# Matrix transposes written as products with the identity, in a graph network kernel

## The chip, the cores and the metric

One core of one Trainium2 chip runs the whole program. The metric is the time of one execution on the device in microseconds (us). The engines are called PE (TensorE), DVE (VectorE), ACT (ScalarE), POOL (GpSimd) and SP (SyncE, which only issues transfers here). PEld is PE's weight load, which the profile lists beside the products.

## The reference

Two message passing layers over a graph of 6250 nodes and 206250 edges, sorted by the node that they end in. A node has 64 scalars and 32 vectors of 3 components (160 numbers). All is float32.

```python
# layer 0, per edge (attention)
msg_s = (s_n @ Ws_src)[src] + (s_n @ Ws_dst)[dst]          # and the same for the vectors
w1 = rbf @ W_rbf                                           # 16 -> 224, the radial product
m1_s, m1_v = _cg_tp(msg_s, msg_v, y0, y1, w1[...])         # products with y0, y1: outer, dot, cross
a = (m1_s @ W_alpha).reshape(e, H, AS_)                    # the logits, softmax over the edges of a node
val_s, val_v = m1_s @ Ws_val, einsum(m1_v, Wv_val) * sigmoid(val_s @ Wg)
m2_s, m2_v = _cg_tp(sigmoid(val_s), val_v, y0, y1, w2...)
h = concat(m2_s @ Ws_vlin, einsum(m2_v, Wv_vlin))
agg = segment_sum(alpha * h, dst)                          # then node + agg @ Wps, Wpv, and a norm
# layer 1, per edge (convolution)
w = edge_query @ tp_weight                                 # 64 -> 224
edge_x = products of w, h[edge_src] and edge_sh            # 352 numbers (outer, dot, cross)
agg = segment_sum(edge_x, edge_dst)                        # then two linear maps, and a norm
```

## The kernel before

The program runs seven stages one after the other, each a block with its own instruction streams. Their order by time is: `attention_input` (norm of the nodes and the two tables that edges gather from, 49 blocks of 128 nodes), `attention_edges` (404 groups of 512 edges), `segment_softmax`, `attention_aggregate` (452 steps), `attention_output` (49 blocks), `conv_edges` (452 steps of 512 edges), `conv_output` (49 blocks).

Features of edges or nodes lie with the edge or node on the partition. To multiply them by a weight matrix, PE needs them turned, with the feature on the partition. So each such product is preceded by PE transposes of 128 rows into PSUM, and by a copy of the turned block to SBUF on ACT.

In `attention_edges` the work on one group of 512 edges (four sub-blocks k of 128 edges) is spread over several passes of a loop body. PE's body, in the order of the code, is: `turn(t,0)`, `values_of(t,0)`, `turn(t,1)`, `turn(t,2)`, `values_of(t,1)`, `maps(t,0)`, `turn2(t,0)`, the radial product (L681), `turn2(t,1)`, `maps(t,1)`, `turn2(t,2)`, where the t of each belongs to another group of edges. Each `turn` (L614) and `turn2` (L623) is four transposes, one for each k. `maps` (L631 to L633) is six products with 200, 96 and 96 columns twice over; `values_of` (L641 to L643) is six products with 96 columns. ACT copies each turned block of 128 by 512 (L709, L713). DVE adds the gathered rows (L570), forms outer products with y (L498, L550), cross and dot products (L512 to L527), and multiplies with the radial weights in PSUM (L531 to L540, after which `first_done` goes up). PE's radial product waits for `first_done` of the group before, since `b_w` is not double buffered. DVE forms `rbfy` (L521) from two halves of a loaded tile `rin`.

In `conv_edges` PE sums the edges of a node by products with a 0/1 matrix (L1331, L1333) and multiplies the queries (L1343). DVE does the outer products with y in three instructions on line L1269 (diag, plus, minus), the cross and dot products (L1283 to L1285), a copy of y to PSUM (L1290), and more. Nothing there is transposed.

All waits are written out by hand with semaphores. Each engine takes its instructions in the order of the code.

Of the kernel before, what the change touches and what calls it, by code (L numbers as in the profile page):

```python
# [21 lines left out]
ALU = mybir.AluOpType  # L22
# [5 lines left out]
P = 128  # L28
# [20 lines left out]
    ("ones", 128, 128), ("count", 128, STEPS), ("sidx", 128, 4),  # L49
    ("iota", 128, 128), ("wy", 64, WY), ("m1_0", 128, 200), ("m1_1", 128, 96), ("m1_2", 96, 96), ("val_t", 64, 128),  # L50
# [97 lines left out]
def attention_input(nc, g):  # L148
# [6 lines left out]
    with ExitStack() as ctx:  # L155
# [27 lines left out]
        with nc.Block() as block:  # L183
# [155 lines left out]
            @block.tensor  # L339
            def _(pe):  # L340
                pe.wait_ge(chain, 4)
                for c in range(4):
                    ins = pe.matmul(banks[6][:, 0:STEPS], w("ones"), begun[:, c, :], start=(c == 0), stop=(c == 3))
                ins.then_inc(summed, 1)
                for m in range(BLOCKS + 1):
                    if m < BLOCKS:
                        pe.wait_ge(phase, 8 * chunk_of[m] + 8)
                        wait(pe, kept, m - 1)
                        pe.transpose(b_t[m % 2][0:CS, 0:P], normed[:, m, 0:CS], w("ident"))
                        pe.transpose(b_t[m % 2][0:V3, P:2 * P], normed[:, m, CS:C], w("ident")).then_inc(turned, 1)  # L350
# [12 lines left out]


def attention_edges(nc, g):

    w, psum, banks, io = g["w"], g["psum"], g["banks"], g["io"]
    with ExitStack() as ctx:
# [10 lines left out]
        gdst = [sb(f"gdst{u}", [P, 4, C]) for u in range(4)]  # L379
        rin = [sb(f"rin{u}", [64, 512]) for u in range(4)]  # L380
        rbfy = [sb(f"rbfy{u}", [64, 256]) for u in range(2)]
        msg = sb("msg", [P, 4, C])
# [46 lines left out]
        with nc.Block() as block:  # L429
# [47 lines left out]
            def _(dve):  # L477
# [10 lines left out]
                def body(m):  # L488
# [26 lines left out]
                    if t.inside(SUPER):  # L515
                        dve.wait_ge(early_in[t.slot4], 16 * (t.quarter + 1))
                        wait(dve, outer_done, t.n)
                        dve.tensor_copy(ya, y_early[t.slot4][:, :, 1:6]).then_inc(ya_done, 1)
                        dve.wait_ge(rin_in[t.slot4], 16 * (t.quarter + 1))
                        wait(dve, pe_weights, t.n - 1)  # L520
                        dve.tensor_tensor(rbfy[t.slot][:, :], rin[t.slot4][:, 0:256], rin[t.slot4][:, 256:512], ALU.mult)\  # L521
                            .then_inc(spread, 1)
# [87 lines left out]
            def _(pe):  # L610
                def turn(t, b):
                    lo, rows = P * b, V3 if b == 2 else P
                    for k in range(4):
                        ins = pe.transpose(b_t[b % 2][0:rows, P * k:P * k + P], first[t.slot][:, k, lo:lo + rows], w("ident"))  # L614
                    ins.then_inc(pe_turned, 1)

                def turn2(t, b):
                    for k in range(4):
                        if b < 2:
                            what = second[t.slot][:, k, P * b:P * b + P]  # L620
                        else:
                            what = gated[t.slot4][:, k, 8:12, :].rearrange("p b c -> p (b c)")
                        ins = pe.transpose(b_t[(b + 1) % 2][:, P * k:P * k + P], what, w("ident"))  # L623
                    ins.then_inc(pe_turned2, 1)
# [21 lines left out]
                def body(m):  # L646
# [29 lines left out]
                    if t.inside(SUPER):  # L676
                        pe.wait_ge(spread, t.n + 1)
                        wait(pe, first_done, t.n)
                        for k in (0, 2, 1, 3):
                            q, e = 32 * (k // 2), P * (k % 2)  # L680
                            ins = pe.matmul(b_w[:, k, :], rbfy[t.slot][q:q + 32, e:e + P], w("wy")[q:q + 32, :], start=True, stop=True)  # L681
                        ins.then_inc(pe_weights, 1)
# [331 lines left out]
def attention_output(nc, g):  # L1014
# [3 lines left out]
    with ExitStack() as ctx:  # L1018
# [18 lines left out]
        with nc.Block() as block:  # L1037
# [88 lines left out]
            def _(pe):  # L1126
                for m in range(BLOCKS + LAG + 1):
                    b = m
                    if b < BLOCKS:
                        pe.wait_ge(shared, 3 * (b // 7) + 3)  # L1130
                        wait(pe, u_kept, b - 1)
                        pe.transpose(bt_u[b % 2][0:V3, 0:P], agg[:, b, 0:V3], w("ident"))
                        pe.transpose(bt_u[b % 2][0:V3, P:2 * P], agg[:, b, CS:C], w("ident")).then_inc(u_turned, 1)
                    b = m - LAG
                    if 0 <= b < BLOCKS:
                        pe.wait_ge(phase, 8 * (b // 7) + 8)
                        wait(pe, t_kept, b - 1)
                        pe.transpose(bt_t[b % 2][0:V3, 0:P], nodes[:, b, 0:V3], w("ident"))
                        pe.transpose(bt_t[b % 2][0:V3, P:2 * P], nodes[:, b, CS:C], w("ident")).then_inc(t_turned, 1)
                    b = m - 1  # L1140
# [44 lines left out]
def conv_edges(nc, g):  # L1185
# [3 lines left out]
    with ExitStack() as ctx:  # L1189
# [6 lines left out]
        idx = [idx_ring[:, u] for u in range(8)]  # L1196
        y_ring = sb("y", [P, 8, 4, 6])
        y = [y_ring[:, u] for u in range(8)]
# [7 lines left out]
        plain = [sb(f"plain{u}", [P, 4, P]) for u in range(4)]  # L1206
        diag, plus = sb("diag", [P, 4, 3, CV]), sb("plus", [P, 4, 3, CV])
        cross, dot = sb("cross", [P, 4, 3, CV]), sb("dot", [P, 4, CV])
# [8 lines left out]
        minus = banks[6][:, 0:384].rearrange("p (k x c) -> p k x c", k=4, x=3)  # L1217
        yp = [banks[6][:, 384 + 24 * u:408 + 24 * u].rearrange("p (k j) -> p k j", k=4) for u in range(2)]
        iota = banks[7][:, 0:P]
# [4 lines left out]
        with nc.Block() as block:  # L1224
            @block.sync
            def _(sp):
                def body(t):

                    step_loads(sp, t, g["step_s"], ((scaled, t.n - 7), (weights, t.n - 7), (plain_done, t.n - 7)),
                               ((idx[t.slot8][:, :], io["eidx"], loaded[t.slot8]),  # L1230
                                (y[t.slot8][:, :, :].rearrange("p k j -> p (k j)"), io["ey6"], loaded[t.slot8]),
                                (query[t.slot8][:, :], io["query"], loaded[t.slot8])))
# [15 lines left out]
            def _(dve):  # L1248
# [4 lines left out]
                def body(m):  # L1253
                    t = m
                    if t.inside(STEPS):
# [31 lines left out]
                    if t.inside(STEPS):  # L1287
                        dve.wait_ge(loaded[t.slot8], 48 * (t.eighth + 1))
                        wait(dve, outer_done, t.n - 1)
                        dve.tensor_copy(yp[t.slot], y[t.slot8][:, :, :]).then_inc(turned_y, 1)  # L1290
                        wait(dve, summed, t.n - 3)
# [57 lines left out]
def conv_output(nc, g):  # L1349

    w, banks, agg, nodes, io = g["w"], g["banks"], g["agg1"], g["nodes"], g["io"]
    with ExitStack() as ctx:
# [12 lines left out]
        with nc.Block() as block:  # L1365
# [94 lines left out]
def lay_pack(i):  # L1460
# [12 lines left out]
    ss, sv, vs, vv0, vv1 = rbf[:, :64], rbf[:, 64:128], rbf[:, 128:160], rbf[:, 160:192], rbf[:, 192:224]  # L1473
    for lo in (0, 32):
        W["wy"][lo:lo + 16, 0:64], W["wy"][lo:lo + 16, 192:224] = ss, vs
        W["wy"][lo + 16:lo + 32, 64:128], W["wy"][lo + 16:lo + 32, 128:160], W["wy"][lo + 16:lo + 32, 160:192] = sv, vv0, vv1
    for name in ("gamma_s", "beta_s"):
# [42 lines left out]
def lay_inputs(i):  # L1520
# [15 lines left out]

    rbf = np.pad(np.asarray(i["edge_attr_16"]), ((0, E - EDGES), (0, 0))).reshape(SUPER, 2, 256, 16).transpose(0, 1, 3, 2)
    y0 = np.broadcast_to(y[:, :, 0].reshape(SUPER, 2, 1, 256), rbf.shape)
    left = np.concatenate([rbf, rbf], 2).reshape(SUPER, 64, 256)
    right = np.concatenate([y0, np.ones_like(rbf)], 2).reshape(SUPER, 64, 256)  # L1540
    query = np.pad(np.asarray(i["edge_attr_64"]), ((0, E - EDGES), (0, 0))).reshape(SUPER, 2, 256, 64)
    query = query.transpose(0, 1, 3, 2).reshape(SUPER, P, 256)
    return dict(
        pack=lay_pack(i), x=x, eidx=eidx, ey6=ey6, sdst=sdst, dst3=dst3,
        rin=np.concatenate([left, right], 2), yall=y.reshape(4 * SUPER, P, 4).transpose(1, 0, 2),
# [21 lines left out]
```

## Time and profile before

| what | value |
|---|---|
| median of 3 runs | 7991.2 us (7987.54 to 7993.15) |
| profiled execution | 7987.12 us, of which its span 7985.3 us |
| DVE busy | 7640.4 us, 96% of the span |
| PE busy | 7044.2 us, 88% |
| PE weight loads | 5904.8 us, 74% |
| ACT busy | 5259.3 us, 66% |
| POOL busy | 5304.9 us, 66% |
| mean granted clock of PE | 0.967 of 2.4 GHz |

The span runs from the first to the last instruction; the execution is 1.8 us longer. PE busy counts the modelled ends of pipelined matmuls, so it is more than the time in which the array takes columns: the starts of successive matmuls tell the rate. Shares over the whole span are means over seven stages, so the stages are looked at one by one.

### The profile page before, as it was taken

How to read it: one execution, taken by the hardware profiler on the slowest of the kernel's cores; microseconds unless marked ns; L12 is line 12 of the kernel's file. 1: busy time of each engine (PE TensorE's matmuls, PEld its weight loads, DVE VectorE, ACT ScalarE, POOL GpSimd, SP SyncE). 2: the span in 40 equal slices, each digit the busy share in tenths (PEclk: the TensorE clock that was granted, in tenths of full speed). 3: DMA queues.
4: the chain of work that ended last, by engine and by line, in shares of the span. 5: the costliest groups of instructions: out<-in, count | busy, mean ns of one | idle time of the engine just before them, and what ended most of it. 6: DMA issues, size and time to landing. Idle time of an engine off the chain costs nothing. (4 is left out here: it accounts for less than half of the span.)

```text
span 7985.3 us, 199893 instructions
## 1 busy us (share of the span) xinstructions
PE 7044.2 (88%) x48227; PEld 5904.8 (74%) x48227; DVE 7640.4 (96%) x19067; ACT 5259.3 (66%) x18286; POOL 5304.9 (66%) x5500
## 2 busy tenths in 40 slices
PE   6899999999999999999999859998888888888888
PEld 4888888888888888888888848875555555555556
DVE  5999999999999999999999889976999999999999
ACT  2666666666666666666666634435777777777775
POOL 2777777777777777777777426634777777777772
PEclk5999999999999999999999979977999999999999
DMA  3444344433443333443333337732333333333332
GB/s 104 107 109 105 105 106 105 106 105 104 106 105 106 105 105 106 105 106 105 105 106 106 84 130 261 258 115 69 93 89 90 89 89 88 89 89 89 90 89 58
DMA packets 789804, 854.44 MB, mean 107 GB/s; under 512 B 413920, under 2 KB 571488, under 8 KB 789216
## 3 DMA queue, kind: packets, MB, share of 16 engines
q0 software_dynamic: 241920, 413.20, 21.2%
q1 hardware_dynamic: 547232, 436.34, 18.3%
q10 hardware_dynamic: 576, 4.01, 0.1%
q8 instruction: 33, 0.54, 0.0%
q14 instruction: 43, 0.35, 0.0%
HBM read 704.54 MB, written 148.44 MB: 107 GB/s over the span
## 5 line engine op out<-in xcount | busy, mean ns | idle before, releaser
L1242 POOL DMA_INDIRECT agg<-tab_conv,ce_idx x1808 | 1708.7, 945 | 866.5 <-issue 616.0
L468 POOL DMA_INDIRECT ae_gsrc<-tab_src,ae_idx x1616 | 1533.5, 949 | 751.3 <-issue 446.9
L471 POOL DMA_INDIRECT ae_gdst<-tab_dst,ae_idx x1616 | 1645.9, 1019 | 539.6 <-issue 539.6
L1331 PE MATMUL psum<-ce_prod,ce_plain 128*128 128x384 f32 x3616 | 1539.7, 508 | 328.5 <-DVE ce_prod L1304 275.7
L1316 ACT ACTIVATE ce_prod<-ce_raw,ce_y 128x64 f32<-128x64 f32 x5424 | 1463.8, 332 | 0.0
L1314 ACT ACTIVATE ce_prod<-ce_raw,ce_y 128x160 f32<-128x160 f32 x1808 | 752.2, 416 | 514.5 <-DVE ce_raw L1263 514.5
L713 ACT ACTIVATE ae_second_t<-psum 128x512 f32<-128x512 f32 x1212 | 732.1, 604 | 507.3 <-PE psum L623 500.1
L1333 PEld LDWEIGHTS psum<-ce_prod,ce_plain 128*128 128x128 f32 x3616 | 687.7, 190 | 479.5 <-issue 1.5
L1331 PEld LDWEIGHTS psum<-ce_prod,ce_plain 128*128 128x128 f32 x3616 | 546.9, 191 | 475.4 <-DVE ce_plain L1292 345.5
L631 PE MATMUL psum<-pack_sb,ae_first_t 128*128 128x200 f32 x3232 | 850.1, 345 | 2.2 <-ACT ae_first_t L709 2.0
L641 PE MATMUL psum<-pack_sb,ae_second_t 128*128 128x96 f32 x3232 | 664.4, 287 | 129.1 <-ACT ae_second_t L713 126.6
L709 ACT ACTIVATE ae_first_t<-psum 128x512 f32<-128x512 f32 (+1 forms) x1212 | 692.1, 610 | 41.1 <-PE psum L614 40.9
L681 PE MATMUL psum<-pack_sb,ae_rbfy 32*128 32x224 f32 x3232 | 417.4, 372 | 303.0 <-DVE ae_first L540 281.2
L641 PEld LDWEIGHTS psum<-pack_sb,ae_second_t 128*128 128x128 f32 x3232 | 486.0, 190 | 241.4 <-issue 164.0
L614 PE MATMUL psum<-pack_sb,ae_first 128*128 128x128 f32 (+1 forms) x4848 | 662.9, 273 | 0.8 <-ACT ae_first_t L709 0.8
L719 ACT ACTIVATE ae_values<-psum 128x256 f32<-128x256 f32 x808 | 310.2, 384 | 522.2 <-PE psum L643 522.2
L1333 PE MATMUL psum<-ce_prod,ce_plain 128*128 128x96 f32 x3616 | 646.8, 261 | 0.0
L948 POOL TENSOR_TENSOR ag_exval<-ag_val,ag_wide 128x384 f32<-128x384 f32 x452 | 385.2, 852 | 381.3 <-DMA ag_val<-h_dram 190.7
L633 PE MATMUL psum<-pack_sb,ae_first_t 96*128 96x96 f32 x3232 | 625.9, 275 | 0.0
L643 PE MATMUL psum<-pack_sb,ae_second_t 128*128 128x96 f32 x3232 | 625.4, 275 | 0.0
L642 PE MATMUL psum<-pack_sb,ae_second_t 128*128 128x96 f32 x3232 | 625.3, 275 | 0.0
L765 ACT ACTIVATE ae_second<-agg,ae_y_late 128x192 f32<-128x192 f32 x1616 | 598.3, 444 | 0.0
(217 smaller groups left out, 18692.7 us busy)
## 6 DMA issues: line engine op xcount, KB each, us to landing
ag_val<-h_dram SPq DMA_DIRECT2D x452, 320.0 KB, 4.1
h_dram<-ae_hout SPq DMA_DIRECT2D x404, 320.0 KB
agg<-in_query SPq DMA_DIRECT2D x452, 128.0 KB
ae_rin<-in_rin SPq DMA_DIRECT2D x404, 128.0 KB
agg<-tab_conv,ce_idx POOLq DMA_INDIRECT x1808
ae_gsrc<-tab_src,ae_idx POOLq DMA_INDIRECT x1616
ae_gdst<-tab_dst,ae_idx POOLq DMA_INDIRECT x1616
ce_idx<-in_eidx SPq DMA_DIRECT2D x452, 4.0 KB
```

Source lines behind the costliest of these rows:

```text
L468: pool.indirect_dma_start(gsrc[t.slot4][:, k, :], None, g["tab_src"], bass.IndirectOffsetOnAxis(ap=idx[t.slot4][:, k:k + 1], axis=0))\
L471: pool.indirect_dma_start(gdst[t.slot4][:, k, :], None, g["tab_dst"], bass.IndirectOffsetOnAxis(ap=idx[t.slot4][:, 4 + k:5 + k], axis=0))\
L614: ins = pe.transpose(b_t[b % 2][0:rows, P * k:P * k + P], first[t.slot][:, k, lo:lo + rows], w("ident"))
L631: pe.matmul(b_m[:, i, 0:200], first_t[0][:, e], w("m1_0"), start=True, stop=False)
L641: pe.matmul(b_h[:, i, 0:96], second_t[0][:, e], w("m2_0"), start=True, stop=False, skip_group_check=True)
L709: act.activation(first_t[b][0:rows, :], b_t[b % 2][0:rows, :], ACT.Copy).then_inc(kept, 1)
L713: act.activation(second_t[b][:, :], b_t[(b + 1) % 2][:, :], ACT.Copy).then_inc(kept2, 1)
L1242: pool.indirect_dma_start(node[t.slot8][:, k, :], None, g["tab_conv"], bass.IndirectOffsetOnAxis(ap=idx[t.slot8][:, k:k + 1], axis=0))\
L1314: act.activation(prod[t.slot][:, k, 0:160], raw[t.slot][:, k, 0:160], ACT.Identity, scale=y[t.slot8][:, k, 0:1])
L1316: ins = act.activation(prod[t.slot][:, k, 192 + 96 * x:256 + 96 * x], raw[t.slot][:, k, 160:WW], ACT.Identity, scale=y[t.slot8][:, k, x + ...
L1331: pe.matmul(b_a[t.slot], plain[t.slot4][:, k, :], prod[t.slot][:, k, 96:480], start=(k == 0), stop=False, skip_group_check=True)
L1333: ins = pe.matmul(b_a[t.slot][:, 96:384].rearrange("p (x c) -> p x c", x=3)[:, :, CS:96], plain[t.slot4][:, k, :], prod[t.slot][:, k, 0:96 ...
```

## The change

Every `pe.transpose` outside of `segment_softmax` becomes `pe.matmul` with the same operands: the data as stationary matrix and the identity as moving one. The radial product takes `rbfy` from 128 partitions instead of 64: two sub-blocks of 128 edges share the columns, and each reads its weights from its own rows and its own half of a wider `wy`, in which the other rows are zero. In `conv_edges` the products for diag and plus are one DVE instruction, for which y is loaded with eight numbers per edge (a new input `ey8`) instead of six.

```diff
-                        pe.transpose(b_t[m % 2][0:CS, 0:P], normed[:, m, 0:CS], w("ident"))
+                        pe.matmul(b_t[m % 2][0:CS, 0:P], normed[:, m, 0:CS], w("ident"), start=True, stop=True)
...
-        rin = [sb(f"rin{u}", [64, 512]) for u in range(4)]
-        rbfy = [sb(f"rbfy{u}", [64, 256]) for u in range(2)]
+        rin = [sb(f"rin{u}", [P, 2 * P]) for u in range(4)]
+        rbfy = [sb(f"rbfy{u}", [P, P]) for u in range(2)]
...
-                        dve.tensor_tensor(rbfy[t.slot][:, :], rin[t.slot4][:, 0:256], rin[t.slot4][:, 256:512], ALU.mult)\
+                        dve.tensor_tensor(rbfy[t.slot][:, :], rin[t.slot4][:, 0:P], rin[t.slot4][:, P:2 * P], ALU.mult)\
...
-                        ins = pe.transpose(b_t[b % 2][0:rows, P * k:P * k + P], first[t.slot][:, k, lo:lo + rows], w("ident"))
+                        ins = pe.matmul(b_t[b % 2][0:rows, P * k:P * k + P], first[t.slot][:, k, lo:lo + rows], w("ident"), start=True, stop=True)
...
-                        ins = pe.transpose(b_t[(b + 1) % 2][:, P * k:P * k + P], what, w("ident"))
+                        ins = pe.matmul(b_t[(b + 1) % 2][:, P * k:P * k + P], what, w("ident"), start=True, stop=True)
...
-                            q, e = 32 * (k // 2), P * (k % 2)
-                            ins = pe.matmul(b_w[:, k, :], rbfy[t.slot][q:q + 32, e:e + P], w("wy")[q:q + 32, :], start=True, stop=True)
+                            q, half = slice(64 * (k // 2), 64 * (k // 2) + 64), WY * (k % 2)
+                            ins = pe.matmul(b_w[:, k, :], rbfy[t.slot][q, :], w("wy")[q, half:half + WY], start=True, stop=True)
...
-                        pe.transpose(bt_u[b % 2][0:V3, 0:P], agg[:, b, 0:V3], w("ident"))
+                        pe.matmul(bt_u[b % 2][0:V3, 0:P], agg[:, b, 0:V3], w("ident"), start=True, stop=True)
...
-                        pe.transpose(bt_t[b % 2][0:V3, 0:P], nodes[:, b, 0:V3], w("ident"))
+                        pe.matmul(bt_t[b % 2][0:V3, 0:P], nodes[:, b, 0:V3], w("ident"), start=True, stop=True)
...
-        diag, plus = sb("diag", [P, 4, 3, CV]), sb("plus", [P, 4, 3, CV])
+        both = sb("both", [P, 4, 2, 3, CV])
+        diag, plus = both[:, :, 0, :, :], both[:, :, 1, :, :]
...
-                        for d, out in enumerate((diag[:, :, :, :], plus[:, :, :, :], minus)):
-                            ins = dve.tensor_tensor(out, comps(here[:, :, CS:C]),
-                                                    yp[t.slot][:, :, 1 + d:4 + d].unsqueeze(3).to_broadcast(three), ALU.mult)
-                        ins.then_inc(outer_done, 1)
+                        dve.tensor_tensor(both[:, :, :, :, :].rearrange("p k d x c -> p k d (x c)"),
+                                          here[:, :, CS:C].unsqueeze(2).to_broadcast([P, 4, 2, V3]),
+                                          yp[t.slot][:, :, 0:6].unsqueeze(3).to_broadcast([P, 4, 6, CV]), ALU.mult)
+                        dve.tensor_tensor(minus, comps(here[:, :, CS:C]), yp[t.slot][:, :, 4:7].unsqueeze(3).to_broadcast(three),
+                                          ALU.mult).then_inc(outer_done, 1)
...
-                            ins = pe.transpose(b_t[b % 4][:, P * i:P * i + P], agg[:, b, P * i:P * i + P], w("ident"))
+                            ins = pe.matmul(b_t[b % 4][:, P * i:P * i + P], agg[:, b, P * i:P * i + P], w("ident"), start=True, stop=True)
```

## Rows read from the trace of the kernel before

**Rows 1.** Windows by stage: length, busy time (and instructions) of each engine, granted PE clock, DMA.

```profile
0.00:163.00 163.00, 108.64 (x304) 67.33 (x304) 84.53 (x180) 36.84 (x108) 23.01 (x15) 0.56 0.32 110
163.00:4590.00 4427.00, 4002.96 (x32333) 3687.77 (x32334) 4335.58 (x11313) 2943.88 (x8891) 3172.25 (x3225) 0.99 0.40 104
...
5278.00:5475.00 197.00, 186.52 (x596) 134.21 (x594) 88.65 (x199) 53.73 (x155) 15.78 (x1) 0.51 0.07 22
5475.00:7908.00 2433.00, 2104.06 (x10848) 1434.39 (x10848) 2420.16 (x5876) 1920.96 (x7232) 1708.70 (x1808) 1.00 0.37 88
7908.00:7985.30 77.30, 55.66 (x441) 53.83 (x441) 61.66 (x114) 24.27 (x57) 0.00 (x0) 0.84 0.13 53
```

**Rows 2.** Waits, 1000 to 4000: who waited, for whom, us in total, times, longest.

```profile
PE psum L681 <- DVE ae_first L540: 185.2, 277, 0.8
...
PE psum L641 <- ACT ae_second_t L713: 85.6, 276, 0.3
```

**Rows 3.** Timeline of `attention_edges`, PE's products alone: start, us, what, count.

```profile
2999.91 1.03 PE L681 MATMUL psum<-pack_sb,ae_rbfy 32*128 32x224 f32 x8 [0.61 <-DVE ae_first L540]
...
3002.92 0.60 PE L623 MATMUL psum<-pack_sb,agg 128*128 128x128 f32 x4
...
3003.36 0.60 PE L614 MATMUL psum<-pack_sb,ae_first 128*128 128x128 f32 x4
...
3004.29 0.46 PE L641 MATMUL psum<-pack_sb,ae_second_t 128*128 128x96 f32 x2 [0.33 <-ACT ae_second_t L713]
...
3005.70 1.04 PE L614 MATMUL psum<-pack_sb,ae_first 128*128 128x128 f32 x8
...
3006.57 0.39 PE L641 MATMUL psum<-pack_sb,ae_second_t 128*128 128x96 f32 x2
...
3007.92 0.53 PE L631 MATMUL psum<-pack_sb,ae_first_t 128*128 128x200 f32 x2
...
3009.49 0.60 PE L623 MATMUL psum<-pack_sb,ae_second 128*128 128x128 f32 x4
...
3010.91 1.03 PE L681 MATMUL psum<-pack_sb,ae_rbfy 32*128 32x224 f32 x8 [0.81 <-DVE ae_first L540]
```

**Rows 4.** Groups by line and shape, whole span: count, busy, mean ns, idle before.

```profile
L614 PE MATMUL psum<-pack_sb,ae_first 128*96 128x128 f32 x1616 | 243.0, 273 | 0.8 <-ACT ae_first_t L709 0.8
...
L643 PE MATMUL psum<-pack_sb,ae_second_t 128*128 128x96 f32 x3232 | 625.4, 275 | 0.0
...
L1008 PE MATMUL psum<-ag_exval,ag_hot 128*128 128x164 f32 x3616 | 568.4, 313 | 18.2 <-DVE ag_exval L987 13.0 <-issue 0.2
```

**Rows 5.** Timelines of `attention_aggregate` and `conv_edges`, PE's products.

```profile
5274.77 4.26 PE L1008 MATMUL psum<-ag_exval,ag_hot 128*128 128x164 f32 x27
...
6502.48 0.84 PE L1331 MATMUL psum<-ce_prod,ce_plain 128*128 128x384 f32 x2
...
6503.16 0.36 PE L1333 MATMUL psum<-ce_prod,ce_plain 128*128 128x96 f32 x2
...
6505.18 1.03 PE L1343 MATMUL psum<-pack_sb,agg 64*128 64x224 f32 x8
```

**Rows 6.** Timeline of `conv_edges`, DVE: start, us, what.

```profile
6501.01 0.27 DVE L1304 TENSOR_TENSOR ce_prod<-psum,ce_dot 128x128 f32<-128x128 f32 x1
6501.20 0.67 DVE L1260 TENSOR_TENSOR ce_raw<-psum,agg 128x512 f32<-128x512 f32 x1
6501.80 0.54 DVE L1263 TENSOR_TENSOR ce_raw<-psum,agg 128x384 f32<-128x384 f32 x1
```

**Rows 7.** Timeline of PE where `attention_edges` begins, at the lower clock.

```profile
183.36 2.89 PE L614 MATMUL psum<-pack_sb,ae_first 128*128 128x128 f32 x12
...
192.21 1.86 PE L681 MATMUL psum<-pack_sb,ae_rbfy 32*128 32x224 f32 x8 [1.92 <-DVE ae_first L540]
```

**Rows 8.** Windows there (columns as in the first group): the granted clock rises.

```profile
196.00:197.00 1.00, 1.00 (x6) 1.00 (x6) 0.00 (x0) 0.00 (x0) 0.69 (x2) 0.50 0.19 50
...
198.00:199.00 1.00, 0.69 (x6) 0.45 (x5) 0.79 (x2) 0.96 (x3) 0.80 (x1) 1.00 0.51 98
```

More of the change, by code:

```diff
@@ L49 @@
     ("ones", 128, 128), ("count", 128, STEPS), ("sidx", 128, 4),
-    ("iota", 128, 128), ("wy", 64, WY), ("m1_0", 128, 200), ("m1_1", 128, 96), ("m1_2", 96, 96), ("val_t", 64, 128),
+    ("iota", 128, 128), ("wy", 128, 2 * WY), ("m1_0", 128, 200), ("m1_1", 128, 96), ("m1_2", 96, 96), ("val_t", 64, 128),
     ("wg", 64, 32), ("adot", 128, 72), ("m2_0", 128, 96), ("m2_1", 128, 96), ("m2_2", 128, 96),
@@ L348, in _ @@
                         wait(pe, kept, m - 1)
-                        pe.transpose(b_t[m % 2][0:CS, 0:P], normed[:, m, 0:CS], w("ident"))
-                        pe.transpose(b_t[m % 2][0:V3, P:2 * P], normed[:, m, CS:C], w("ident")).then_inc(turned, 1)
+                        pe.matmul(b_t[m % 2][0:CS, 0:P], normed[:, m, 0:CS], w("ident"), start=True, stop=True)
+                        pe.matmul(b_t[m % 2][0:V3, P:2 * P], normed[:, m, CS:C], w("ident"), start=True, stop=True).then_inc(turned, 1)
                     b = m - 1
@@ L1131, in _ @@
                         wait(pe, u_kept, b - 1)
-                        pe.transpose(bt_u[b % 2][0:V3, 0:P], agg[:, b, 0:V3], w("ident"))
-                        pe.transpose(bt_u[b % 2][0:V3, P:2 * P], agg[:, b, CS:C], w("ident")).then_inc(u_turned, 1)
+                        pe.matmul(bt_u[b % 2][0:V3, 0:P], agg[:, b, 0:V3], w("ident"), start=True, stop=True)
+                        pe.matmul(bt_u[b % 2][0:V3, P:2 * P], agg[:, b, CS:C], w("ident"), start=True, stop=True).then_inc(u_turned, 1)
                     b = m - LAG
@@ L1137, in _ @@
                         wait(pe, t_kept, b - 1)
-                        pe.transpose(bt_t[b % 2][0:V3, 0:P], nodes[:, b, 0:V3], w("ident"))
-                        pe.transpose(bt_t[b % 2][0:V3, P:2 * P], nodes[:, b, CS:C], w("ident")).then_inc(t_turned, 1)
+                        pe.matmul(bt_t[b % 2][0:V3, 0:P], nodes[:, b, 0:V3], w("ident"), start=True, stop=True)
+                        pe.matmul(bt_t[b % 2][0:V3, P:2 * P], nodes[:, b, CS:C], w("ident"), start=True, stop=True).then_inc(t_turned, 1)
                     b = m - 1
@@ L1196, in conv_edges @@
         idx = [idx_ring[:, u] for u in range(8)]
-        y_ring = sb("y", [P, 8, 4, 6])
+        y_ring = sb("y", [P, 8, 4, 8])
         y = [y_ring[:, u] for u in range(8)]
@@ L1217, in conv_edges @@
         minus = banks[6][:, 0:384].rearrange("p (k x c) -> p k x c", k=4, x=3)
-        yp = [banks[6][:, 384 + 24 * u:408 + 24 * u].rearrange("p (k j) -> p k j", k=4) for u in range(2)]
+        yp = [banks[6][:, 384 + 28 * u:412 + 28 * u].rearrange("p (k j) -> p k j", k=4) for u in range(2)]
         iota = banks[7][:, 0:P]
@@ L1230, in body @@
                                ((idx[t.slot8][:, :], io["eidx"], loaded[t.slot8]),
-                                (y[t.slot8][:, :, :].rearrange("p k j -> p (k j)"), io["ey6"], loaded[t.slot8]),
+                                (y[t.slot8][:, :, :].rearrange("p k j -> p (k j)"), io["ey8"], loaded[t.slot8]),
                                 (query[t.slot8][:, :], io["query"], loaded[t.slot8])))
@@ L1289, in body @@
                         wait(dve, outer_done, t.n - 1)
-                        dve.tensor_copy(yp[t.slot], y[t.slot8][:, :, :]).then_inc(turned_y, 1)
+                        dve.tensor_copy(yp[t.slot], y[t.slot8][:, :, 1:8]).then_inc(turned_y, 1)
                         wait(dve, summed, t.n - 3)
@@ L1473, in lay_pack @@
     ss, sv, vs, vv0, vv1 = rbf[:, :64], rbf[:, 64:128], rbf[:, 128:160], rbf[:, 160:192], rbf[:, 192:224]
-    for lo in (0, 32):
-        W["wy"][lo:lo + 16, 0:64], W["wy"][lo:lo + 16, 192:224] = ss, vs
-        W["wy"][lo + 16:lo + 32, 64:128], W["wy"][lo + 16:lo + 32, 128:160], W["wy"][lo + 16:lo + 32, 160:192] = sv, vv0, vv1
+    for lo in (0, 32, 64, 96):
+        own = W["wy"][lo:lo + 32, WY * (lo // 32 % 2):]
+        own[0:16, 0:64], own[0:16, 192:224] = ss, vs
+        own[16:32, 64:128], own[16:32, 128:160], own[16:32, 160:192] = sv, vv0, vv1
     for name in ("gamma_s", "beta_s"):
@@ L1535, in lay_inputs @@
     ey6 = y.reshape(SUPER, 4, P, 4)[..., [0, 1, 2, 3, 1, 2]].transpose(0, 2, 1, 3).reshape(SUPER, P, 24)
[L1537 to L1540, printed above, removed]
+    ey8 = y.reshape(SUPER, 4, P, 4)[..., [0, 1, 2, 3, 2, 3, 1, 2]].transpose(0, 2, 1, 3).reshape(SUPER, P, 32)
+    rbf = np.pad(np.asarray(i["edge_attr_16"]), ((0, E - EDGES), (0, 0))).reshape(SUPER, 4, P, 16).transpose(0, 1, 3, 2)
+    y0 = np.broadcast_to(y[:, :, 0].reshape(SUPER, 4, 1, P), rbf.shape)
+    left = np.concatenate([rbf, rbf], 2).reshape(SUPER, P, P)
+    right = np.concatenate([y0, np.ones_like(rbf)], 2).reshape(SUPER, P, P)
     query = np.pad(np.asarray(i["edge_attr_64"]), ((0, E - EDGES), (0, 0))).reshape(SUPER, 2, 256, 64)
@@ L1543, in lay_inputs @@
     return dict(
-        pack=lay_pack(i), x=x, eidx=eidx, ey6=ey6, sdst=sdst, dst3=dst3,
+        pack=lay_pack(i), x=x, eidx=eidx, ey6=ey6, ey8=ey8, sdst=sdst, dst3=dst3,
         rin=np.concatenate([left, right], 2), yall=y.reshape(4 * SUPER, P, 4).transpose(1, 0, 2),
```

## The prediction

> **What bounds the kernel now.** I cut the span into its stages first [rows 1], since a share over the whole span hides who waits. `attention_edges` is more than half of it: 4427 us, in which DVE is busy for 4336 us (98%) and PE for 4003 us (90%). DVE sets the pace and PE is close behind. `conv_edges` is 2433 us with DVE busy for 2420 us. `attention_input` (163 us) and `attention_output` (197 us) run with a mean granted clock of 0.56 and 0.51, so PE is mostly at its lower level of 1.2 GHz, and in `attention_output` PE is busy for 187 of 197 us. `conv_output` has both levels (mean 0.84). The aggregation and the softmax aren't touched.
>
> The list of waits names two on PE in `attention_edges`: for DVE's `first_done` before the radial product, 185 us, and for ACT's copy before `values_of`, 86 us [rows 2]. The first comes once in each group of 512 edges, 277 times in 3000 us, so a group takes 10.83 us. To see how much room PE has I took one group from the timeline and went by starts, since the durations contain pipelined ends [rows 3]. From one radial product to the next it is 11.00 us there. Four transposes take 0.44 us (3002.92 to 3003.36) and eight take 0.87 us, so PE stood idle from 3003.80 to 3004.29 and from 3009.93 to 3010.91, 1.47 us. PE's own work is 11.00 - 1.47 = 9.53 us a group. Of it the 24 transposes are 24 x 0.11 = 2.64 us, and the rest 6.89 us.
>
> **The change, part by part.**
>
> *Transposes in `attention_edges`.* A transpose leaves one matmul record: the third block of `first`, 4 x 404 = 1616 transposes, shows x1616. A plain float32 product leaves two: L643, also 1616 in the code, shows x3232 [rows 4]. So each turned block becomes two passes, each with its weight load. What a pass with 128 moving columns costs no row at full clock shows. From below: passes with 96 columns follow each other in (3007.92 - 3006.57)/12 = 0.1125 us [rows 3], closer to the 0.11 us of a transpose than to their columns, so the weight load of 128 columns, the same here, is what they wait for. From above: 164 columns take (4.26 - 0.31)/26 = 0.152 us, with 0.31 us for the end of the last; 384 columns take (6503.16 - 6502.48)/2 = 0.34 us [rows 4, 5]. The line through these two falls by 0.00085 us a column and gives 0.152 - 36 x 0.00085 = 0.121 us at 128. That is above the bound of the load, so I take it. The 48 passes are 5.81 us, and PE's work is 6.89 + 5.81 = 12.70 us a group.
>
> DVE needs 10.83 us less what is saved below, so PE becomes the bound. Its old stalls go. The four transposes of `turn(t,0)` now last 0.97 us and cover ACT's copy (0.77 us from the end of `turn2` at 3003.52 to the start of `values_of` at 3004.29). `first_done` comes before PE needs it, since DVE has 1.9 us to spare in each group. So a group takes 12.70 us: 404 x (12.70 - 10.83) = **+755 us**. At 0.1125 us a pass it is 6.89 + 5.40 = 12.29 us and +590 us; at 0.152 us it is 14.19 us and +1357 us.
>
> The Trainium skill (TensorE: Matmul & The Clock Gate, section Terms) says of the transpose mode that it is four times faster for FP32. That speaks against this change more strongly than the rows do, which give 0.242 against 0.11 us, a factor of 2.2. By the page's factor a turned block would take 0.44 us and the stage 2675 us more.
>
> *Radial product.* `rbfy` goes from 256 to 128 elements a partition. In DVE's timeline 128 elements take 0.19 us to the next start and 512 take 0.60 us [rows 6], so 128 elements less are 0.137 us, 55 us over 404 groups. With PE as the bound they are hidden in DVE's new idle time: 0. They count if DVE stays the bound. On PE nothing: eight passes with 64 rows and 224 columns in `conv_edges` take 1.03 us [rows 5], as the eight with 32 rows do [rows 3]. The transfers have the same bytes over twice the partitions, at a DMA share of 0.40 [rows 1].
>
> *y products merged in `conv_edges`.* Two instructions of 384 elements become one of 768. By rows 6 the fixed part of one is 0.19 - 0.137 = 0.05 to 0.06 us, and 452 x 0.06 = **-27 us**, all of it on the path, since DVE is busy for 99% of the stage [rows 1]. The copy of y grows by 4 elements, 2 us in all; the loads of y are 4 KB larger, against a DMA share of 0.37. Bounds: 0 and -40 us.
>
> *`conv_output`.* 147 transposes become 294 passes. PE's part grows by 147 x (0.242 - 0.11) = 19 us, but DVE is busy for 62 of 77 us [rows 1] and PE waits part of the time: **+10 us**, between 0 and 25 us.
>
> *`attention_input` and `attention_output`.* Here the clock decides. At 1.2 GHz a transpose takes twice its 0.11 us (twelve are in 2.89 us with the end of the last [rows 7]), and a second pass another 0.22 us, so 98 blocks add 22 us and 196 add 43 us, nearly all on PE's path. But where `attention_edges` begins, PE did 12 transposes from 183.36 us and the granted clock was still 0.50 at 196 us; after the run of plain products that begins at 192.21 us it had gone to 1.00 by 198 us [rows 7, 8]. With the transposes gone both stages are nothing but plain products, so I expect the upper level for most of them. In `attention_output` PE's work of 187 + 43 us would halve to 115 us, beside 89 us of DVE and hand-overs to ACT that don't shrink; I take 150 us, **-45 us**. In `attention_input` PE's 109 + 22 us would become 65 us, less than DVE's 85 us [rows 1]; of the 163 us I take off **-30 us**.
>
> The Trainium skill (same page, Part 4: PE-mode transpose) says that transposes don't engage the upper clock level, because they aren't counted as PE being busy. The start of `attention_edges` agrees. With the rule these two stages give -75 us, without it +65 us.
>
> *Sum.* 755 - 27 + 10 - 30 - 45 = +663 us against the profiled execution's 7987.1 us (2 us over its span, 4 under the median): 8650, with the median 8654. I say **8650 us**.
>
> **Rivals.**
> 1. *The same, but the clock stays low in the two node stages.* For it: both run at the lower level although most of their passes are plain already. The sum is 755 - 27 + 10 + 22 + 43 = +803, 8790 us.
> 2. *The passes are bound by the load alone*, 0.1125 us each, and 128 columns hide behind it as 96 do. 590 - 92 = +498, 8485 us.
> 3. *Four times* a transpose, 0.44 us for a turned block, as if two records stood for slower passes than any row's. 2675 - 92 = +2583, 10570 us. Against it are 384 columns in 0.34 us.
> 4. *Faster: PE stays under DVE.* If a product with the identity costs little more than a transpose, DVE keeps the pace at 10.83 - 0.14 = 10.69 us. It decides at 10.69 - 9.53 = 1.16 us of growth a group, 0.05 us a transpose. Then -55 - 27 - 75 = -157, 7830 us. Against it are the two records [rows 4]; for it only that 128 columns aren't measured.
>
> **Numbers.** Forecast 0.58, rival 1 0.24, rival 2 0.11, rival 3 0.01, rival 4 0.03, and 0.03 for passes near 0.152 us (about 9250 us). The range takes in rivals 1 and 2, with some 0.002 us a pass beyond the one and 0.007 us beyond the other (0.001 us a pass is 48 x 404 x 0.001 = 19 us): 8450 to 8930 us. A measurement of this kernel can tell about 0.2% from no change. Slower has 0.96, within 0.2% 0.01, faster 0.03.
>
> **What would show it.** In the changed kernel L614 and L623 must show 9696 matmuls each against 4848 now, with as many weight loads; PE's wait for L540 before L681 must be nearly gone; DVE must show long waits for PE and ACT and fall to about 83% busy in `attention_edges`; a group must take 12.7 us. L1269 must show two shapes, the new one near 0.94 us. The granted clock in the node stages tells the forecast from rival 1. I am wrong if a group takes under 10.8 us, or if a turned block's two passes take other than 0.22 to 0.27 us, or if PE keeps waits of a microsecond a group, for which DVE's chain from `maps` over the gate to `first_done` would be the place.

## The result

The changed kernel takes 8678.97 us (median of 4 runs, 8673.51 to 8685.35), the kernel before 7992.17 us beside it: a ratio of 1.0862, 95% interval 1.0848 to 1.0876. It is slower by 687 us. The forecast was 8650 us.

Cut into stages as in [rows 1], the changed kernel's windows are (length, busy time of PE, PEld, DVE, ACT, POOL, granted clock, DMA share, GB/s):

```profile
0.00:197.00 197.00, 147.62 (x402) 83.57 (x402) 84.64 (x180) 37.45 (x108) 22.38 (x14) 0.54 0.27 92
197.00:5258.00 5061.00, 5033.87 (x42008) 4853.05 (x42009) 4322.16 (x11310) 3080.52 (x8887) 3314.07 (x3226) 1.00 0.34 91
...
5950.00:6191.00 241.00, 232.36 (x820) 189.19 (x819) 93.65 (x210) 55.23 (x163) 18.33 (x4) 0.52 0.06 17
6191.00:8600.00 2409.00, 2104.03 (x10848) 1434.34 (x10848) 2394.57 (x5424) 1920.91 (x7232) 1713.53 (x1808) 1.00 0.37 90
8600.00:8678.00 78.00, 66.29 (x588) 66.00 (x588) 61.95 (x114) 25.04 (x57) 0.00 (x0) 0.95 0.13 53
```

In `attention_edges` PE and DVE have changed places: PE is busy for 5034 of 5061 us, DVE for 4322. The two node stages stayed at the lower clock (0.54 and 0.52) and grew.

For exact lengths I take the start of each stage's first product (L681, L1008, L1132, the query product, the first turned block of `conv_output`) and the span's end. In us, with the terms of the prediction:

| stage | before | after | difference | forecast |
|---|---|---|---|---|
| `attention_input` | 168.8 | 203.4 | +34.6 | -30 |
| `attention_edges` with the softmax | 4536.6 | 5178.0 | +641.4 | +755 |
| `attention_aggregate` | 576.6 | 577.0 | +0.4 | 0 |
| `attention_output` | 193.1 | 233.8 | +40.7 | -45 |
| `conv_edges` | 2433.7 | 2408.7 | -25.0 | -27 |
| `conv_output` | 76.5 | 77.2 | +0.7 | +10 |
| sum | 7985.3 | 8678.1 | +692.8 | +663 |

The sum is right to 30 us because two errors, of -114 us in the edge stage and +150 us in the node stages, lie on opposite sides. That is luck: neither stage came out as forecast, and the prediction gave no reason why the two should cancel.

PE's timeline of one group in the changed kernel (start, us, what, count), to be read against [rows 3]:

```profile
3002.83 0.39 PE L641 MATMUL psum<-pack_sb,ae_second_t 128*128 128x96 f32 x2
...
3003.50 1.96 PE L614 MATMUL psum<-pack_sb,ae_first 128*128 128x128 f32 x16
3005.30 0.36 PE L641 MATMUL psum<-pack_sb,ae_second_t 128*128 128x96 f32 x2
...
3008.19 1.08 PE L623 MATMUL psum<-pack_sb,ae_second 128*128 128x128 f32 x8
3009.20 1.03 PE L681 MATMUL psum<-pack_sb,ae_rbfy 64*128 64x224 f32 x8
3010.16 1.16 PE L623 MATMUL psum<-pack_sb,ae_second 128*128 128x128 f32 x8
3011.16 0.50 PE L631 MATMUL psum<-pack_sb,ae_first_t 128*128 128x200 f32 x2
```

No product waits: 16 passes of 128 columns start (3005.30 - 3003.50)/16 = 0.1125 us after each other, as passes of 96 columns do. A set of eight beside another kind of work takes longer, up to 1.01 us (3008.19 to 3009.20). From the first L681 to the last, 203.4 to 5212.1 us, 403 groups pass, 12.43 us each. The two waits of PE of [rows 2] are gone, and DVE and ACT wait instead. From the list of waits, 1000 to 4000 us:

```profile
ACT ae_second_t L713 <- PE psum L623: 437.6, 602, 1.3
DVE agg L505 <- ACT ae_mapped L704: 391.1, 241, 1.7
POOL ae_gsrc L468 <- DVE ae_msg L570: 374.0, 181, 2.1
```

The counts answer to [rows 4]. L614 and L623 show 9696 matmul records each, as forecast. A turned block of the third kind, x1616 before, is now two passes:

```profile
L614 PE MATMUL psum<-pack_sb,ae_first 128*96 128x128 f32 x3232 | 419.1, 273 | 0.0
```

### The profile page after: what moved, and what is told of

Read it like the earlier page. It is cut to its first block and busy times, and to the rows that moved or that the text cites. A ratio compares the mean times of both kernels' runs of the same rounds, so it can differ in the third digit from the quotient of the medians.

```text
span 8678.1 us, 219715 instructions
## 1 busy us (share of the span) xinstructions
PE 8170.9 (94%) x58364; PEld 7153.8 (82%) x58364; DVE 7604.2 (88%) x18615; ACT 5399.3 (62%) x18286; POOL 5451.5 (63%) x5500
## 5 line engine op out<-in xcount | busy, mean ns | idle before, releaser
L468 POOL DMA_INDIRECT ae_gsrc<-tab_src,ae_idx x1616 | 1644.4, 1018 | 1269.4 <-DVE ae_msg L570 582.9
L471 POOL DMA_INDIRECT ae_gdst<-tab_dst,ae_idx x1616 | 1676.4, 1037 | 542.4 <-issue 541.8
L614 PE MATMUL psum<-pack_sb,ae_first 128*128 128x128 f32 (+1 forms) x9696 | 1218.6, 276 | 0.0
L614 PEld LDWEIGHTS psum<-pack_sb,ae_first 128*128 128x128 f32 (+1 forms) x9696 | 1130.8, 183 | 0.6 <-issue 0.5
L709 ACT ACTIVATE ae_first_t<-psum 128x512 f32<-128x512 f32 (+1 forms) x1212 | 735.4, 607 | 291.8 <-PE psum L614 291.8
L623 PE MATMUL psum<-pack_sb,ae_second 128*128 128x128 f32 x6464 | 904.6, 283 | 0.0
L623 PEld LDWEIGHTS psum<-pack_sb,ae_second 128*128 128x128 f32 x6464 | 784.1, 191 | 111.3 <-issue 111.3
L505 DVE TENSOR_TENSOR agg<-ae_mapped,agg 128x512 f32<-128x512 f32 x404 | 279.8, 693 | 658.6 <-ACT ae_mapped L704 658.6
L641 PE MATMUL psum<-pack_sb,ae_second_t 128*128 128x96 f32 x3232 | 639.0, 279 | 5.1 <-ACT ae_second_t L713 2.9
L642 PE MATMUL psum<-pack_sb,ae_second_t 128*128 128x96 f32 x3232 | 625.4, 275 | 0.0
```

The lines of the kernel that those rows point to most:

```text
L468: pool.indirect_dma_start(gsrc[t.slot4][:, k, :], None, g["tab_src"], bass.IndirectOffsetOnAxis(ap=idx[t.slot4][:, k:k + 1], axis=0))\
L471: pool.indirect_dma_start(gdst[t.slot4][:, k, :], None, g["tab_dst"], bass.IndirectOffsetOnAxis(ap=idx[t.slot4][:, 4 + k:5 + k], axis=0))\
L614: ins = pe.matmul(b_t[b % 2][0:rows, P * k:P * k + P], first[t.slot][:, k, lo:lo + rows], w("ident"), start=True, stop=True)
L623: ins = pe.matmul(b_t[(b + 1) % 2][:, P * k:P * k + P], what, w("ident"), start=True, stop=True)
L709: act.activation(first_t[b][0:rows, :], b_t[b % 2][0:rows, :], ACT.Copy).then_inc(kept, 1)
```

## The experiments

### First four runs, on a disturbed machine

In the runs of this group the kernel before itself took 12026 us (median of 17, from 11826 to 20129), against 7991 us elsewhere. The engines wait up to 20.6 us at a time, where the longest wait in the list above is 2.1 us. Why is not known. So the whole times are not set against the expectations; the shortest groups of edges are, those between the disturbances. Undisturbed, the shortest group of a kernel is a little under its mean, 10.80 against 10.85 us in the kernel before.

The edits are the ones of the change's diff, in part: in the first only lines 614 and 623 are as after, in the second only they are as before, in the third all transposes are as before, in the fourth all but those of line 614 are.

> The kernel before with only the turned blocks of attention_edges (L614, L623) as plain products; radial product, merged y and the node stages stay as before. Theory A (PE's growth by the second passes sets the whole loss): a group takes 12.4 to 12.5 us as in the changed kernel, the stage is some 640 us longer, time near 8630 us (8610 to 8650). Rival B (the radial product on 128 partitions, with twice the transfer packets, or its wider weights, has a part in the loss): the group takes clearly less, 12.2 us or under, and the time is below 8560 us. The node stages must last as before (first L681 at 169 us).

12448 us, 1.04 (1.0308 to 1.0491) of the kernel before; no group shorter than 14.84 us in 2000 to 3000 us. Nothing follows.

> The changed kernel with the turned blocks of attention_edges back as transposes; the plain products stay in attention_input, attention_output and conv_output. Theory A: attention_edges is bound by DVE again and gains 404 x 0.137 = 55 us by the smaller rbfy; the node stages keep their loss, +35 us in attention_input, +41 in attention_output, +1 in conv_output, at the lower clock; conv_edges keeps -25. Sum -4 us, time near 7983 us (7970 to 8000). Rival B (the first stage is cold only because of what comes after, or PE's room is too small for the smaller rbfy to count): 8030 us or more.

11909 us, 0.995 (0.991 to 0.999). The shortest of 55 groups there took 10.68 us (start to start of L521), so DVE is the bound again, as theory A has it. Its sum for the node stages stays undecided, as this kernel was not timed without the disturbance.

> The changed kernel with every transpose back as a transpose: what is left is the radial product on 128 partitions and the merged y products. Theory A: -55 us in attention_edges (a group 10.69 us), -25 us in conv_edges (a step 5.33 to 5.30 us), nothing else: 7912 us (7895 to 7925). Rival B (the saving on rbfy is lost in the chain from maps over the gate to first_done, since PE and ACT waits are part of the group's time): a group stays above 10.8 us and the time is near 7965 us.

11837 us, 0.987 (0.979 to 0.995). Here too the shortest groups took 10.68 us, near theory A's 10.69 us. Two waits of this run between 1000 and 4000 us show how long the disturbances were:

```profile
POOL ae_gsrc L468 <- DVE ae_msg L570: 1212.4, 108, 20.6
ACT ae_values L719 <- remote: 654.4, 109, 14.4
```

> As the variant without products, but the 12 turned blocks of L614 in each group of attention_edges are plain products (L623 stays transposes). PE's own work is then 9.53 + 12 x 0.1125 = 10.9 to 11.1 us a group, just above DVE's 10.69 us. Theory A (PE's work and DVE's work, whichever is longer): a group takes 11.0 to 11.2 us, 404 x 0.4 = 160 us over the variant without products, near 8070 us (8030 to 8110). Rival B (PE keeps part of its waits of about 1 us a group, since the order of the waits costs something by itself): a group takes 11.6 us or more, 8270 us or more. Rival C (half of the loss of 24 blocks, linear): 404 x 0.87 = 350 us over it, 8265 us.

11818 us, 0.988 (0.979 to 0.996), shortest group 11.48 us. Undecided; the first, third and fourth were run again.

### Without any plain product

> The variant without products once more (radial product and merged y kept, every transpose a transpose), since in the first runs of these variants the kernel before took about 12000 us, so that its whole-run times are not comparable with the result. Theory A: a group 10.68 us, a step of conv_edges 5.30 us, 7912 us (7895 to 7925) where the kernel before takes 7991. Rival B: the group stays above 10.8 us and the time is near 7965 us.

7920.0 us (7915.8 to 7921.9), 0.9915 (0.9898 to 0.9931) of the kernel before at 7989.2. By stages: `attention_edges` with the softmax 4491.6 us (-45), `conv_edges` 2407.7 us (-26), the others as before. Theory A holds, with a group of 10.74 us instead of 10.68 and so 45 us for the smaller `rbfy` instead of 55.

### Only the edge stage's blocks as products

> The kernel before with only the turned blocks of attention_edges as plain products, once more, for a time beside a kernel before of 7990 us. Theory A (the second passes alone set the loss): a group takes 12.4 to 12.5 us as in the changed kernel, 8630 us (8610 to 8650). Rival B (the radial product on 128 partitions has a part in the loss): a group of 12.2 us or less and below 8560 us.

8631.85 us, 1.0803 (1.0783 to 1.0822). Its first L681 and first L1008 (start of the stage to start of the next) against those of the changed kernel:

```profile
L681 PE MATMUL psum<-pack_sb,ae_rbfy x3232: 345/348/737, 168.7 to 5176.1; 32*128 32x224 f32 x191
...
L1008 PE MATMUL psum<-ag_exval,ag_hot x3616: 302/303/613, 5346.2 to 5919.5; 128*128 128x164 f32 x191
```

```profile
L681 PE MATMUL psum<-pack_sb,ae_rbfy x3232: 347/350/739, 203.4 to 5212.1; 64*128 64x224 f32 x191
...
L1008 PE MATMUL psum<-ag_exval,ag_hot x3616: 302/303/613, 5381.4 to 5955.2; 128*128 128x164 f32 x191
```

5177.5 us here, 5178.0 us there: the products on lines 614 and 623 are the whole loss of the stage, and the radial product, in the one with 32 rows and in the other with 64, costs and gains nothing while PE is the bound. The same edit gains 45 us while DVE is.

### Half of the blocks

> The variant without products, with the 12 turned blocks of L614 in a group as plain products, once more. In the disturbed run its shortest group was 11.48 us. Theory A (PE's work 9.53 + 12 x 0.1125 + small, nothing else): 11.0 to 11.2 us a group, near 8090 us. Rival B (PE keeps part of its waits): 11.5 us or more a group, 8250 us or more.

8017.0 us, 1.0037 (1.0024 to 1.0050) of the kernel before, and 97 us over the variant without products. The stage's window (columns as above) shows PE without a gap, and DVE nearly so:

```profile
1000.00:4000.00 3000.00, 3000.00 (x25134) 2865.57 (x25134) 2922.87 (x7651) 2051.29 (x6012) 2189.61 (x2185) 1.00 0.39 104
```

From its first L681 to its last (166.8 to 4592.0 us) a group takes 10.98 us. With 0, 12 and 24 blocks as products a group takes 10.74, 10.98 and 12.43 us. The first twelve cost 0.24 us, the second twelve 1.45 us, 0.12 us a block: a bend, not a line, so rival C falls, and so does B, since PE kept no wait. The value lies a little under A's 11.0 to 11.2, and 73 us under its later 8090 us: 9.53 + 12 x 0.1125 = 10.88 us needed only 0.10 us on top.

### What keeps the node stages at the lower clock

In these, products and blocks are given more rows; the added ones meet weights that are zero, so each result is the same. The edits are shown against the variant without products. First `attention_output` with 128 features in each turned block and 128 rows in each product, transposes kept:

```diff
-                        pe.transpose(bt_u[b % 2][0:V3, 0:P], agg[:, b, 0:V3], w("ident"))
-                        pe.transpose(bt_u[b % 2][0:V3, P:2 * P], agg[:, b, CS:C], w("ident")).then_inc(u_turned, 1)
+                        pe.transpose(bt_u[b % 2][:, 0:P], agg[:, b, 0:P], w("ident"))
+                        pe.transpose(bt_u[b % 2][:, P:2 * P], agg[:, b, CS - 32:C], w("ident")).then_inc(u_turned, 1)
...
-                        pe.matmul(bo_u[b % 2][:, 0:CS], feat_u[b % 2][0:CS, 0, :], w("wps"), start=True, stop=True)
+                        pe.matmul(bo_u[b % 2][:, 0:CS], feat_u[b % 2][:, 0, :], w("wps"), start=True, stop=True)
```

> As the variant without products, but in attention_output every turned block is 128 features wide and every product uses 128 rows (the added rows meet zero weights, so the result is the same). Theory C (what keeps attention_output at the lower clock is that its products use 64 and 96 rows, and differ in shape from one to the next; that a part of them are transposes does not matter): the stage leaves the lower level, lasts 110 to 160 us instead of 193, and the time is 35 to 80 us below that of the variant without products. Rival D (the short waits between the dependent steps keep it low whatever the rows): granted clock 0.50, the stage 180 to 200 us, the time within 15 us of the variant without products. attention_input is unchanged in both and must last as before.

7838.95 us, 0.9814 (0.9798 to 0.9831), 81 us under the variant without products, one more than theory C's 80. Its windows in this stage:

```profile
5253.00:5263.00 10.00, 8.02 (x35) 6.66 (x34) 8.51 (x18) 2.67 (x8) 0.00 (x0) 0.50 0.00 0
5263.00:5283.00 20.00, 16.83 (x125) 15.54 (x125) 18.16 (x42) 9.12 (x32) 0.00 (x0) 0.98 0.10 30
5283.00:5303.00 20.00, 16.66 (x128) 15.33 (x127) 17.11 (x42) 9.45 (x33) 0.00 (x0) 1.00 0.15 46
```

The stage lasts 113.4 us instead of 193.2, most of it at 2.4 GHz, with the transposes still there.

The same with the four blocks of this stage as plain products:

> The variant with 128 rows in attention_output, but with that stage's turned blocks as plain products instead of transposes (all other transposes stay). Theory C (rows and one shape decide over the clock, not the kind of instruction): the upper level as with transposes; 196 second passes of 0.11 us are 22 us of PE, of which DVE's waits cover a part, so 0 to 22 us slower than 7839 us. Rival E (plain products count for the clock and transposes don't): the stage's start, still at the lower level for some 20 us with transposes, reaches the upper level sooner and the time is below 7839 us.

7846.41 us, 0.9817 (0.9801 to 0.9833); the stage lasts 122.0 us, 8.6 more. Its windows give a granted clock of 0.77 for 5260 to 5280 us and then 1.00, no earlier than with transposes. Theory C, and not E.

Next only the depth of the 64-row products, with transposes and 96 features kept:

```diff
-                        pe.matmul(bo_u[b % 2][:, 0:CS], feat_u[b % 2][0:CS, 0, :], w("wps"), start=True, stop=True)
+                        pe.matmul(bo_u[b % 2][:, 0:CS], feat_u[b % 2][0:V3, 0, :], w("wps"), start=True, stop=True)
...
-                        pe.matmul(both[:, :, 0:CS], feat_t[b % 2][0:CS, 0, :], w("ts1").rearrange("p (o c) -> p o c", o=2),
+                        pe.matmul(both[:, :, 0:CS], feat_t[b % 2][0:V3, 0, :], w("ts1").rearrange("p (o c) -> p o c", o=2),
```

> The variant without products, with only the 64-row products of attention_output made 96 rows deep (zero weights in the added rows), so that all blocks and products there have 96 rows but never 128. Theory F (the change of shape from 64 to 96 rows, with its unhidden weight loads, is what keeps the clock low): stage at the upper level, 110 to 140 us, time 7840 to 7865. Theory G (the rows themselves: below 128 it stays low): granted clock 0.50, stage 165 to 193 us (less only by the gaps that vanish), time 7890 to 7920 us.

7847.21 us, 0.9819 (0.9804 to 0.9835), and 117.0 us for the stage, at a granted clock of 1.00 from 5270 to 5338 us. These are theory F's numbers, not G's. Two instructions per block, 64 rows deep instead of 96, cost the kernel 73 us. PE's weight loads, still at the lower clock, where the sums are easiest to see; first of the kernel before, then of this variant:

```profile
5303.11 0.50 PEld L1144 LDWEIGHTS psum<-pack_sb,ao_feat_u 64*128 64x128 f32 x2 [0.44 <-issue]
5303.73 0.50 PEld L1145 LDWEIGHTS psum<-pack_sb,ao_feat_u 96*128 96x128 f32 x2
```

```profile
5256.21 0.50 PEld L1144 LDWEIGHTS psum<-pack_sb,ao_feat_u 96*128 96x128 f32 x2 [0.40 <-issue]
5256.60 0.55 PEld L1145 LDWEIGHTS psum<-pack_sb,ao_feat_u 96*128 96x128 f32 x2
```

From the load for the 64-row product to the next one it is 0.62 us, and 0.39 us with 96 rows. In a steady stretch at the lower clock a whole block of nodes shows it too; first the kernel before, then this variant:

```profile
5340.60 0.42 PE L1132 MATMUL psum<-pack_sb,agg 128*96 128x128 f32 x1
...
5344.40 0.42 PE L1132 MATMUL psum<-pack_sb,agg 128*96 128x128 f32 x1
```

```profile
5266.86 0.42 PE L1132 MATMUL psum<-pack_sb,agg 128*96 128x128 f32 x1
...
5269.63 0.38 PE L1132 MATMUL psum<-pack_sb,agg 128*96 128x128 f32 x1
```

A block takes 3.80 us before and 2.77 us here at the same clock. So 49 x 1.03 = 50 us of the stage are the uncovered loads themselves, and the rest of its 76 us comes with the higher clock. Whether the clock follows from the uncovered stretches or from the 64-row products as such is not separated: no run has 64 rows in all products of a stage. Against the second stands `conv_edges`, where products with 64 rows run at a granted clock of 1.00 among others with 128 [rows 1, 5].

### The same question in the changed kernel's first stage

In `attention_input` of the changed kernel the first block is 64 features wide and its product 64 rows deep, the second 96. Here both have 96:

```diff
-                        pe.matmul(b_t[m % 2][0:CS, 0:P], normed[:, m, 0:CS], w("ident"), start=True, stop=True)
+                        pe.matmul(b_t[m % 2][0:V3, 0:P], normed[:, m, 0:V3], w("ident"), start=True, stop=True)
```

> The changed kernel, with the first turned block of attention_input 96 features wide instead of 64, and its product 96 rows deep, so that no weight load there changes its shape. Theory H (the weight load is not hidden where the width or depth changes from one product to the next, which made a block cost 0.87 us more instead of 0.43): a block takes about 2.3 to 2.5 us instead of 2.95 and the stage is 22 to 32 us shorter than 203 us. Rival: the plain pass itself is slower in this stage, and the block stays at 2.9 us.

8610.23 us (one run), 69 us under the changed kernel's median, and its first L681 is at 133.1 us instead of 203.4. The direction is theory H's, but the gain of 70 us is over twice its 22 to 32 us. The loads of the changed kernel show why its blocks took 2.95 us, with an idle stretch before each change, all of which are to or from 64 rows or 64 columns:

```profile
101.74 0.50 PEld L358 LDWEIGHTS psum<-pack_sb,ai_feat 96*128 96x128 f32 x2 [0.23 <-issue]
102.68 0.29 PEld L349 LDWEIGHTS psum<-pack_sb,ai_normed 128*64 128x64 f32 x2 [0.44 <-issue]
103.30 0.40 PEld L350 LDWEIGHTS psum<-pack_sb,ai_normed 128*96 128x96 f32 x2 [0.33 <-issue]
103.97 0.28 PEld L356 LDWEIGHTS psum<-pack_sb,ai_feat 64*128 64x128 f32 x1 [0.28 <-issue]
```

In the variant, also at the lower clock, they are gone:

```profile
48.26 0.60 PEld L349 LDWEIGHTS psum<-pack_sb,ai_normed 128*96 128x96 f32 x2
48.79 0.50 PEld L350 LDWEIGHTS psum<-pack_sb,ai_normed 128*96 128x96 f32 x2
49.22 0.55 PEld L356 LDWEIGHTS psum<-pack_sb,ai_feat 96*128 96x128 f32 x2
49.65 0.55 PEld L358 LDWEIGHTS psum<-pack_sb,ai_feat 96*128 96x128 f32 x2
```

A block takes 1.92 us here (46.34 to 48.26, first load to first load), 1.03 us less than 2.95, where theory H said 2.3 to 2.5 us. The loads still alternate between 128 rows with 96 columns and 96 rows with 128 columns, as they do in the variant of `attention_output` before this one. So not every change of shape leaves a load uncovered; of those tried here, the ones to or from 64 do. The rest of the gain is the clock, which theory H had left out. Two windows of the variant:

```profile
60.00:80.00 20.00, 15.68 (x109) 14.66 (x109) 15.72 (x36) 9.85 (x30) 0.00 (x0) 0.93 0.38 116
80.00:100.00 20.00, 17.42 (x105) 16.54 (x104) 15.94 (x35) 9.39 (x28) 0.00 (x0) 0.80 0.32 100
```

### A version better than both

The variant without products, with 128 rows in both node stages:

> The variant with 128 rows in attention_output, and attention_input treated likewise (blocks of 128 features, 128 rows in every product, zero weights in the rest). Theory C: attention_input leaves the lower level after its start and loses 30 to 60 of its 168 us: 7780 to 7810 us. Rival D (DVE's norm chain and ACT's two copies per block bound it once PE is faster): within 20 us of 7839 us.

7799.14 us (7793.82 to 7802.72), 0.9758 (0.9744 to 0.9772) of the kernel before, within theory C's range, and the fastest kernel here. The first L681 is at 126.3 us instead of 168.2, `attention_output` takes 113.3 us. DVE now shares the bound in `attention_input`: it is busy for 16 of every 20 us there, as the clock moves between both levels (0.72 to 0.83).

## Why the prediction came out

**Right in mechanism: the edge stage.** PE had 1.2 us of room a group, the second passes took 2.7, and the place of the bound moved to PE. The edges-only variant shows that nothing else is in it, and the bend between 12 and 24 blocks that a group takes PE's work or DVE's, whichever is longer. PE kept no waits, as said. DVE is busy for 2579 of 3000 us (86%, forecast 83%).

**Mis-sized: a pass of 128 columns.** "The line through these two falls by 0.00085 us a column and gives 0.152 - 36 x 0.00085 = 0.121 us at 128." In a run of like passes it is 0.1125 us, the lower bound that the prediction had. With 0.1125 the sum gave 12.29 us a group and +590 us; measured are 12.43 us and +641. In the group that begins at 3000.24 us, 12.47 us long, the 48 passes take 5.66 us by starts, 0.118 us each, since sets of eight beside another kind of work take 0.92 to 1.01 us instead of 0.90; the rest of PE's work is 6.81 us instead of 6.89. So the forecast's 0.121 us came near the mean, though not for its reason. What bounds a pass at 128 columns is not shown: the weight load may, as the prediction has it, but the columns alone would give the same, 0.34 x 128/384 = 0.113 us by [rows 5].

**Wrong: the clock of the node stages.** "With the transposes gone both stages are nothing but plain products, so I expect the upper level for most of them." The granted clock stayed at 0.54 and 0.52, and the term of -75 us came out as +75. Rival 1 described this, at +65. Rival 1 and rival 2 together, 590 - 27 + 10 + 65 = +638 us, describe what was measured, +693 us, better than the forecast does in either stage.

The prediction read [rows 7, 8] as a sign that the kind of instruction matters. They are none. When the clock rose at 198 us PE had already turned to transposes again:

```profile
197.15 1.41 PE L614 MATMUL psum<-pack_sb,ae_first 128*128 128x128 f32 x8
```

And in the variant with 128 rows and plain products in `attention_output`, whose first two stages do the same work as those of the variant without products, the clock rose right behind the first 12 transposes:

```profile
182.51 1.86 PE L681 MATMUL psum<-pack_sb,ae_rbfy 64*128 64x224 f32 x8 [10.86 <-DVE ae_first L540]
184.31 2.82 PE L614 MATMUL psum<-pack_sb,ae_first 128*128 128x128 f32 x12
```

```profile
186.00:187.00 1.00, 1.00 (x6) 0.64 (x4) 0.00 (x0) 0.66 (x2) 0.69 (x2) 0.54 0.34 82
187.00:188.00 1.00, 0.32 (x2) 0.20 (x2) 0.00 (x0) 0.59 (x1) 0.87 (x1) 1.00 0.33 82
```

So behind the same eight products and 12 transposes the clock rises at once in one trace and ten microseconds later in another. The experiments take kind and shape apart: `attention_output` leaves the lower level with transposes once no product has 64 rows (113 and 117 us), it does so no sooner with plain products of the same shapes (122 us), and with the 64-row products it stays there with transposes (193 us) and without them (234 us). The Trainium skill's statement that transposes don't engage the upper level (TensorE: Matmul & The Clock Gate, Part 4) did not decide here: the stage ran at a granted clock of 0.98 to 1.00 with four transposes in each block. In `attention_input` a block also cost 0.87 us more (2.95 against about 2.09), twice the 0.44 us forecast, because as plain products the blocks' loads of 64 and 96 columns weren't hidden either; 49 x 0.87 would be 43 us, of which 35 came, as PE waits for DVE at the stage's start.

**Four times a transpose.** The Trainium skill (TensorE: Matmul & The Clock Gate, section Terms) has the transpose mode four times faster for FP32. The trace does not agree: it shows a factor of 2.05, 0.225 against 0.11 us for a turned block of 128 by 128.

**Small terms.** The merged y products gave -25.0 us (-27); their instruction lasts 1.04 us by its record instead of 0.94, but 0.86 us to the next start. The radial product gave nothing in the changed kernel, as said, and 45 us (55) where DVE is the bound. `conv_output` lost 0.7 us instead of 10: PE is busy for 66.3 us instead of 55.7, but the granted clock rose from 0.84 to 0.95. Whether the one paid for the other was not tried by itself.

## What to carry to other kernels

Before a transpose is written as a product, count its passes and the other engine's lead: the room here was about 0.05 us a block, the second pass took 0.11. Where a stage runs at the lower clock, look at the shapes in the order of PE's queue before anything else: products that alternate between 64 and 96 rows left the weight load uncovered, and filling them up with rows of zeros to 96 or 128 took 69 to 81 us off the kernels here. A clock that rises behind one kind of instruction doesn't show that the kind did it; look at a second run. A forecast's sum can be right with two terms wrong; compare stage by stage.

## What was not expected of the hardware

A float32 pass with 128 columns follows the next in 0.1125 us, no slower than one with 96, while 164 columns take 0.152 us. At the lower clock a product with 64 rows next to one with 96 costs about a quarter of a microsecond more at each change (3.80 against 2.77 us a block with four changes), and a change between 96 and 128 costs nothing: load to load it is 0.43 us across one (48.79 to 49.22 us) and 0.43 us without one (49.22 to 49.65 us).

In `conv_edges` of the changed kernel DVE's instructions look longer without being later. The timeline of the changed kernel:

```profile
7500.33 1.05 DVE L1269 TENSOR_TENSOR ce_both<-agg,psum 128x768 f32<-128x768 f32 x1
7501.19 0.66 DVE L1272 TENSOR_TENSOR psum<-agg,psum 128x384 f32<-128x384 f32 x1
7501.66 0.65 DVE L1280 TENSOR_TENSOR agg<-agg,psum 128x384 f32 x1
```

384 elements last 0.65 us here and 0.54 in the kernel before [rows 6], but the starts are 0.47 us apart in both. The 768 elements take 0.86 us to the next start, against 0.92 for two of 384. So durations of pipelined DVE instructions are compared by starts. What lengthens the records stays open.
